# A vision block on one core: queries and keys of the first attention projected once and put into blocks by transfers, with new lists

## The reference

```
h  = [cls, rfft2(16x16 patches).real * freq weights @ proj] + pos      # 197 tokens of 192
x1 = layernorm(h)
q, k, v = x1 @ Wq + bq, x1 @ Wk + bk, x1 @ Wv + bv                     # 12 heads of 16
h  = h + concat(softmax(q @ k.T / 4) @ v) @ Wo + bo
x2 = layernorm(h)
gates = softmaxes and a top-2 choice of x2 @ (wg, wg0, wg1)            # a factor for each of 12 heads
q, k, v = x2 @ qkv_w + qkv_b                                           # 12 heads of 64
o  = softmax(layernorm(q) / 8 @ layernorm(k).T) @ v
h  = h + (gates * o) @ proj_w + proj_b
```

## Time and profile before

| | |
|---|---|
| median of three runs | 5198.48 us |
| the profiled execution | 5189.76 us, its span 5188.0 us |
| granted TensorE clock, mean | 0.996 |
| busy share TensorE, weight loads, DVE, ACT, POOL | 97%, 82%, 90%, 85%, 66% |
| DMA | 131.44 MB, 25 GB/s over the span |

### The profile page before, as it was taken

How to read it: one execution, slowest core, us unless ns; L and a number is a source line. 1 busy time by engine, 2 the same in 40 slices (tenths; PEclk the granted TensorE clock), 3 DMA queues, 4 the chain that set the end, 5 groups by cost and what they waited for, 6 DMA issues and landing times.

```text
span 5188.0 us, 196660 instructions
## 1 busy us (share of the span) xinstructions
PE 5021.8 (97%) x61744; PEld 4268.3 (82%) x61744; DVE 4664.9 (90%) x14799; ACT 4402.2 (85%) x17537; POOL 3434.1 (66%) x3462
## 2 busy tenths in 40 slices
...
GB/s 90 20 26 22 22 29 22 22 29 22 22 23 28 22 22 29 22 22 29 22 22 23 29 22 22 29 22 22 29 22 22 22 29 22 22 29 22 22 25 6
DMA packets 69030, 131.44 MB, mean 25 GB/s; under 512 B 8628, under 2 KB 34624, under 8 KB 68704
## 3 DMA queue, kind: packets, MB, share of 16 engines
...
...
## 4 chain that ended last, share of the span: by engine, by line
PE 52%; DVE 35%; issue 11%; DVEq 1%; ACT 0%; POOL 0%; POOLq 0%; ACTq 0%
PE bank L528 42%; PE bank L705 9%; DVE nmax L948 6%; DVE nmax L1047 4%; DVE qkn L1042 4%; DVE v L1024 2%; DVE gfac L1013 2%; DVE qk L943 2%; DVE x L918 2%; DVE oT L1065 2%; DVE h L970 1%; DVE stats L905 1%; DVE ctxT L1060 1%; DVE vs L960 1%; DVE parts L921 1%
## 5 line engine op out<-in xcount | busy, mean ns | idle before, releaser
L512 POOL TENSOR_TENSOR pq<-pq,gn 99x788 f32<-99x788 f32 x768 | 1151.9, 1500 | 756.0 <-DVE gn L1056 742.4
L773 ACT ACTIVATE p<-bank,nmax 99x197 f32<-99x197 f32 x3072 | 1283.5, 438 | 219.4 <-DVE nmax L948 219.4
L811 ACT ACTIVATE pq<-bank,nmax 99x197 f32<-99x197 f32 x3072 | 1287.3, 447 | 137.8 <-DVE nmax L1047 137.8
L1047 DVE TENSOR_REDUCE nmax<-bank 99x2 f32<-99x394 f32 x1536 | 829.8, 561 | 131.0 <-PE bank L528 131.0
L516 POOL TENSOR_TENSOR sq<-qkc 128x396 f32<-128x396 f32 x768 | 644.5, 846 | 364.1 <-ACT qkc L785 364.0
L948 DVE TENSOR_REDUCE nmax<-bank 99x2 f32<-99x394 f32 x1536 | 821.3, 564 | 41.7 <-PE bank L528 38.7
L817 ACT ACTIVATE pT<-bank 99x394 f32<-99x394 f32 x1536 | 740.5, 526 | 66.0 <-PE bank L705 65.9
L528 PE MATMUL bank<-x2T,wqkc 128*128 128x198 f16 (+1 forms) x7680 | 734.1, 249 | 5.7 <-ACT p L773 4.7
L528 PEld LDWEIGHTS bank<-x2T,wqkc 128*128 128x128 f16 (+1 forms) x7680 | 654.8, 98 | 79.6 <-DVE x2T L980 41.0
L705 PE MATMUL bank<-ident,pq 99*99 99x99 f32 (+1 forms) x6144 | 709.6, 254 | 9.0 <-POOL pq L512 7.7
L811 ACT ACTIVATION_READ_ACCUMULATOR pq<-bank,nmax 99x1 f32 x3072 | 700.7, 228 | 0.0
(11 more groups left out here) (155 smaller groups left out, 10335.6 us busy)
## 6 DMA issues: line engine op xcount, KB each, us to landing
xa<-in_xa SPq DMA_DIRECT2D x128, 392.0 KB, 3.1
xb<-in_xb SPq DMA_DIRECT2D x128, 392.0 KB, 3.7
out_tokens<-res SPq DMA_DIRECT2D x128, 74.2 KB
out_tokens<-res SPq DMA_DIRECT2D x128, 73.5 KB
...
```

Source lines behind the costliest of these rows:

```text
L512: nc.gpsimd.tensor_tensor(pair, pair, factor, op=ALU.mult).then_inc(s_sc.up(), 1)
L773: last = nc.scalar.activation(p1[0:TC, h, c, :], psum("s1", h)[0:TC, c * T:c * T + T], ACT.Exp, bias=nmax1[:, c, h:h + 1], accum_out=sum1[ ...
L811: last = nc.scalar.activation(pq[0:TC, h % SLOTS, c, 0:T], psum("s2", h)[0:TC, c * T:c * T + T], ACT.Exp, bias=nmax2[:, h, c:c + 1], accum ...
L1047: V.tensor_reduce(nmax2[:, h, :], psum("s2", h)[0:TC, 0:2 * T].rearrange("p (a b) -> p a b", a=2), op=ALU.max, axis=AX.X, negate=True).the ...
```

## The change

The weights of queries and keys are held once: for a group of four heads 64 columns of queries, then 64 of keys. A qk1 step is one set of five matmuls. ACT writes the high parts of both, DVE the low parts, into a new tile qkhl. When all three groups are there, SP copies qkhl into the blocks of the tile qk1 by 16 transfers within SBUF: for each of the four heads of a group and each half of its 32 rows, one transfer of the queries (high and low, three groups, 16 rows of 3 x 792 bytes) and one of the keys (high for the first half, low for the second, 16 rows of 3 x 396 bytes). Each head has a semaphore, and every s1 step waits for all four. ACT, before it writes qkhl, waits that the transfers of the image before are done and that its s1 steps on TensorE are.

All five lists are new, banks included; SP's gains an entry qx between load and store. Before the loop, ACT makes the high parts of the weights and DVE the low ones; one load of weights goes, and the clearing of v2 moves ahead of the loads.

```
 ORDER = {
     "pe": """
+1:o2_0@0 1:pT_3@5 4:tok@3 2:qk1@6 1:s2_10@05 1:pT_4@2 2:qk2@1 1:pT_5@6 2:qk3@3 3:s1_4@0724 1:o2_1@6 1:o2_2@1 2:qk4@3
+1:pT_6@5 2:qk5@0 1:pT_7@7 3:ctx0@3 2:ms0@0 2:ms1 2:ms2 3:s1_8@2751 1:o2_3@3 1:pT_8@6 2:v2_0@4 1:pT_9@2 3:ctx1@6
+1:pT_10@7 2:rstd0@2 4:x1T@0 2:rstd1@4 1:pT_11@7 1:o2_4@2 1:o2_5@4 2:s2_0@63 2:rstd2@2 4:qk1_0@0 2:v2_1@7 2:v2_2@5
+2:v2_3@1 2:rstd3@4 4:qk1_1@0 3:ctx2@6 2:s2_2@21 4:qk1_2@3 4:v1@0 3:wo@4 2:s2_4@57 1:proj@3 2:pT_0@4 2:rstd4@6 2:pT_1@0
+3:x2T@2 2:s2_6@45 2:rstd5@6 3:qk0@2 2:pT_2@0 4:s1_0@3617 2:s2_8@24
     "dve": """
+4:tok 1:s2_10 1:s2_11 1:gr4 3:ctx0 3:s1_4 3:s1_5 4:nx1 1:ol1 3:s1_6 1:gr5 3:s1_7 1:ol2 3:cl0 3:s1_8 3:s1_9 3:s1_10
+3:ctx1 2:var2 2:v2_0 2:rstd0 2:rstd1 3:cl1 3:s1_11 1:ol3 4:x1T 1:ol4 3:ctx2 2:s2_0 2:rstd2 2:s2_1 1:ol5 4:qk1_0 2:v2_1
+2:v2_2 2:v2_3 2:gl 2:rstd3 2:gate1 4:qk1_1 3:cl2 2:s2_2 2:gate2 2:gate3 2:gr0 4:qk1_2 3:wo 2:s2_3 2:s2_4 3:nx2 2:gr1
+2:rstd4 2:s2_5 3:x2T 2:s2_6 2:rstd5 1:proj 2:s2_7 4:s1_0 4:s1_1 2:s2_8 2:gr2 4:s1_2 2:ol0 4:s1_3 2:s2_9 2:gr3
...
     "sp": """
-4:load 0:store
+4:load 3:qx 0:store
...
-        wqk1 = sb("wqk1", [128, 4, 2 * 3 * 128], F16)
+        wqk1 = sb("wqk1", [128, 4, 3 * 128], F16)
-        qk1 = sb("qk1", [128, 3, 2, 2, TP], F16)
+        qk1 = sb("qk1", [128, 3, 3, TP], F16)
+        qkhl = sb("qkhl", [128, 3, 2, TP], F16)
+        s_qx = [signal(f"qk1_blocks{j}", 64) for j in range(GROUP)]
...
+            def qk_blocks(img, _):
+
+                sp.wait_ge(*read_out(img, "qk1", 2))
+                for j in range(GROUP):
+                    for half in range(2):
+                        dst = slice(32 * j + 16 * half, 32 * j + 16 * half + 16)
+                        sp.dma_start(qk1[dst, :, 0:2, :], qkhl[16 * j:16 * j + 16]).then_inc(s_qx[j].up(16), 16)
+                        sp.dma_start(qk1[dst, :, 2, :], qkhl[64 + 16 * j:80 + 16 * j, :, half, :]).then_inc(s_qx[j].up(16), 16)
+
+            run_phases(sp, "sp", {"qx": qk_blocks, "load": load, "store": store})
...
-                for s in range(2):
-                    w = slice(128 * (3 * s + g), 128 * (3 * s + g) + 128)
-                    last = mm5(o[:, s * TP:s * TP + TP], lambda k, r: wqk1[r, k, w], lambda k, r: x1T[r, k].rearrange("p c n -> p (c n)"), True)
+                w = slice(128 * g, 128 * g + 128)
+                last = mm5(o[:, 0:TP], lambda k, r: wqk1[r, k, w], lambda k, r: x1T[r, k].rearrange("p c n -> p (c n)"), True)
...
-                pe.wait_ge(*read_out(img, "qk1", h // GROUP))
+                for j in range(GROUP):
+                    pe.wait_ge(*s_qx[j].at(img, 64))
...
+            def high_parts(source, dest):
+
+                nc.scalar.activation(dest[:, 0:2], source[:, 0:2], ACT.Copy, scale=W_SCALE)
+                nc.scalar.activation(dest[:, 3], source[:, 2], ACT.Copy, scale=row_scale[:, 0:1]).then_inc(s_high, 1)
...
-                nc.scalar.activation(qk1[:, g, 0, 0, :], psum("qk1", g)[:, 0:TP], ACT.Copy, scale=E1 ** -0.25 / W_SCALE)
-                nc.scalar.activation(qk1[:, g, 0, 1, :], psum("qk1", g)[:, TP:2 * TP], ACT.Copy,
-                                     scale=mask1[:, 0:1]).then_inc(s_qkh.up(), 1)
+                for j in range(GROUP):
+                    act.wait_ge(*s_qx[j].at(img, 0))
+                if not isinstance(img, int) or img > 0:
+                    for h in range(H - GROUP, H):
+                        act.wait_ge(*made(img - 1, "s1", h))
+                nc.scalar.activation(qkhl[:, g, 0, :], psum("qk1", g)[:, 0:TP], ACT.Copy, scale=E1 ** -0.25 / W_SCALE).then_inc(s_qkh.up(), 1)
...
             def split(source, dest):
 
-                link(V.tensor_scalar(dest[:, 0:2], source[:, 0:2], W_SCALE, None, ALU.mult))
-                link(V.tensor_scalar(dest[:, 3], source[:, 2], W_SCALE, bias_rows[:, 0:1], ALU.mult, ALU.mult))
-                link(V.scalar_tensor_tensor(dest[:, 2], source[:, 0], W_SCALE, dest[:, 0], ALU.mult, ALU.subtract))
-                link(V.scalar_tensor_tensor(dest[:, 3], source[:, 2], W_SCALE, dest[:, 3], ALU.mult, ALU.subtract))
+                high[0] += 1
+                dve.wait_ge(s_high, high[0])
+                V.scalar_tensor_tensor(dest[:, 2], source[:, 0], W_SCALE, dest[:, 0], ALU.mult, ALU.subtract)
+                V.scalar_tensor_tensor(dest[:, 3], source[:, 2], W_SCALE, dest[:, 3], ALU.mult, ALU.subtract)
...
-                V.scalar_tensor_tensor(qk1[:, g, 1].rearrange("p a b -> p (a b)"), psum("qk1", g)[:, 0:2 * TP], E1 ** -0.25 / W_SCALE,
-                                       qk1[:, g, 0].rearrange("p a b -> p (a b)"), ALU.mult, ALU.subtract).then_inc(free("qk1", g), 1)
+                V.scalar_tensor_tensor(qkhl[:, g, 1, :], psum("qk1", g)[:, 0:TP], E1 ** -0.25 / W_SCALE,
+                                       qkhl[:, g, 0, :], ALU.mult, ALU.subtract).then_inc(free("qk1", g), 1)
```

More of the change, by code:

```diff
@@ L155 @@
-1:s2_0 3:ctx0 1:s2_1 1:rstd3 0:ol4 2:nx2 3:qk1_1 1:v2_1 1:v2_2 1:rstd4 3:qk1_2 0:ol5 1:v2_3 1:s2_2 2:x2T 3:s1_4 1:s2_3
-1:gl 3:s1_5 1:gate1 1:gate2 1:gate3 3:s1_6 3:cl0 1:gr0 3:s1_7 1:s2_4 1:s2_5 1:gr1 4:tok 1:s2_6 1:s2_7 4:nx1 1:gr2
-0:proj 3:s1_8 3:s1_9 3:s1_10 1:rstd5 3:s1_11 3:ctx1 1:ol0 1:s2_8 1:s2_9 4:x1T 3:ctx2 1:gr3 1:ol1 1:s2_10 3:cl1
+4:tok 1:s2_10 1:s2_11 1:gr4 3:ctx0 3:s1_4 3:s1_5 4:nx1 1:ol1 3:s1_6 1:gr5 3:s1_7 1:ol2 3:cl0 3:s1_8 3:s1_9 3:s1_10
+3:ctx1 2:var2 2:v2_0 2:rstd0 2:rstd1 3:cl1 3:s1_11 1:ol3 4:x1T 1:ol4 3:ctx2 2:s2_0 2:rstd2 2:s2_1 1:ol5 4:qk1_0 2:v2_1
@@ L158 @@
+2:v2_2 2:v2_3 2:gl 2:rstd3 2:gate1 4:qk1_1 3:cl2 2:s2_2 2:gate2 2:gate3 2:gr0 4:qk1_2 3:wo 2:s2_3 2:s2_4 3:nx2 2:gr1
+2:rstd4 2:s2_5 3:x2T 2:s2_6 2:rstd5 1:proj 2:s2_7 4:s1_0 4:s1_1 2:s2_8 2:gr2 4:s1_2 2:ol0 4:s1_3 2:s2_9 2:gr3
 """,
     "act": """
-0:pT_2 0:pT_3 2:s1_8 2:s1_9 2:s1_10 0:o2_0 1:qk4 2:s1_11 1:qk5 0:o2_1 3:x1T 0:s2_8 0:s2_9 2:ctx1 1:var0 1:var1 0:pT_4
-0:s2_10 3:qk1_0 2:ctx2 0:pT_5 0:s2_11 3:v1 0:pT_6 0:o2_2 0:pT_7 0:pT_8 3:s1_0 0:o2_3 3:s1_1 3:s1_2 0:pT_9 0:pT_10
-0:pT_11 3:s1_3 0:o2_4 0:o2_5 1:s2_0 3:qk1_1 4:xhi 1:s2_1 3:qk1_2 2:x2T 1:s2_2 3:s1_4 3:ctx0 1:gate0 1:s2_3 2:qk0
@@ L163 @@
-3:s1_5 2:qk1 3:s1_6 2:qk2 3:s1_7 1:s2_4 1:s2_5 1:pT_0 2:qk3 1:pT_1 1:s2_6 1:s2_7
+0:pT_10 2:s1_10 0:pT_11 3:x1T 0:o2_4 2:s1_11 0:o2_5 4:xhi 3:qk1_0 1:s2_0 1:s2_1 1:gate0 3:qk1_1 2:ctx2 3:qk1_2 1:s2_2
+1:s2_3 3:v1 1:s2_4 1:pT_0 1:pT_1 2:x2T 1:s2_5 1:s2_6 2:qk0 1:pT_2 1:s2_7 3:s1_0 3:s1_1 1:o2_0 1:pT_3 1:s2_8 3:s1_2
+3:s1_3 1:s2_9 2:qk1 1:pT_4 1:s2_10 1:pT_5 2:qk2 1:s2_11 2:qk3 3:s1_4 1:o2_1 3:s1_5 2:qk4 1:o2_2 1:pT_6 2:qk5 3:s1_6
+1:pT_7 3:ctx0 3:s1_7 2:var0 3:s1_8 2:var1 1:pT_8 3:s1_9 1:pT_9 3:ctx1 1:o2_3
@@ L398, in build_vit_block @@
         s_prep = ctx.enter_context(nc.semaphore("prep_vector_step"))
+        s_high = ctx.enter_context(nc.semaphore("weights_high_parts"))
+        s_centred = ctx.enter_context(nc.semaphore("weights_centred"))
         s_pw = ctx.enter_context(nc.semaphore("token_weights_scaled"))
@@ L405, in build_vit_block @@
                        (bias_rows[:], "bias_rows"), (mask1[:], "mask1")]
[L406 removed]
+        first_loads = [(wq1_raw, "wqk1"), (wv1_raw, "wv1"), (wgate_raw, "wgate")]
         second_loads = [(wq_raw, "wq"), (wk_raw, "wk")]
@@ L832, in _ @@
             V.memset(parts[1][:], 1.0)
-            for x in (vs1, ctxT, pq, oT, xh, xl):
+            for x in (vs1, ctxT, pq, oT, xh, xl, v2):
                 V.memset(x[:], 0.0)
@@ L885, in _ @@
             link(V.tensor_scalar(ln_b[:, 0:1], ln_b[:, 0:1], E2 ** -0.5, None, ALU.mult))
-            link(V.memset(v2[:], 0.0))
             dve.wait_ge(s_weff, 6 * KC)
```

52 lines of the change are left out of this document (32 added, 20 removed).

## The result

The changed kernel takes 6024.12 us (median of six runs, 6022.86 to 6025.69), the kernel before 5198.58 beside it: the ratio is 1.1588, interval 1.1573 to 1.1603. The direction was right, the size was not: +826 us where +30 was forecast.

The account below looks back on a forecast made before the run. The prediction took a loop through PE, DVE and SP's transfers as the bound: 15.4 + 15.8 + 7.8 + 0.3 + 0.3 = 39.6 us an image against 39.33, +38 us, less 9 before the loop: 5228 us, range 5110 to 5400.

Parts of the forecast that it names:

- a loop from the third qk1 over SP's transfers to s1_0: Main loop across PE, DVE and SP, closed by the transfers: claimed to set the period at 39.6 us an image.
- DVE's leg: DVE's work from s1_8 to the third qk1 step, put at 15.8 us an image.
- The preparation: Weight preparation before the loop, where ACT takes high parts from DVE: -9 us, bounds 0 to -13.
- The transfers: SP's 16 issues after the third qk1 plus the last landing: 7.8 us, from 7.1 to 12.9.
- the wait that I did forecast: PE at s1_0 waiting for the transfers to land, put at about 0.7 us an image.
- PE's start after the landing: Hand-over from the last transfer's landing to PE's s1_0, estimated at 0.1 us.
- the first term: Time of SP's 16 transfers, issues and last landing, in the loop's sum: 7.8 us, bounds 7.1 to 12.9.
- the second rival: Transfers are dearer, 0.47 us an issue and 2.4 to land, 9.45 in all: 5445 us; chance 0.15.
- PE's total: PE's busy time an image, forecast to fall by 1.3 us from 38.9 to 37.6 through halved projections.
- the third rival: PE bounds the kernel throughout and gives back all that it saves: 5019 us; chance 0.05.
- the first rival: Transfers are hidden, 0.36 us an issue and 7.1 in all: 38.9 us an image, 5138 us; chance 0.32.
- the cover: DVE's steps after the third qk1 until proj, whose bank s1_0 needs, hiding the transfers: 7.1 us.

Follow-up runs that it names:

- the dummies: Changed kernel with 36 matmuls an image that nothing reads, placed ahead of s1_0's wait for the transfers; 5710.41 us, ratio 1.1008.

## Why the prediction was wrong

**Right.** That the end hangs on a loop from the third qk1 over SP's transfers to s1_0, over PE to s1_8 and over DVE back: each link stands in the trace, and taking transfers, DVE steps or the clock's fall out of it moved the time by about the amount that the loop says, as far down as PE's own 38.9 us an image. DVE's leg: 15.8 and 0.1 for the hand-over to SP, 15.9 measured. A qk1 step on PE: 0.435, 0.43 measured (3050.80 to 3051.23). DVE's low parts, by form:

```profile
L980 DVE SCALAR_TENSOR_TENSOR qkhl<-bank,qkhl 128x198 f16<-128x198 f32 x384 | 138.9, 362 | 21.0 <-ACT qkhl L795 5.9
```

against 562 ns in the earlier trace rows. The preparation: -9 us forecast, -12.4 at the memset here and -11 by its own run.

**Wrong.** What failed is the price of an issue, and beside it a term put at nothing, TensorE's clock. By the terms of the sum, 39.6 forecast and 46.6 measured in the image that was read:
1. *The transfers*, 15 x 0.41 + 1.66 = 7.8: measured 15 x 0.64 + 1.9 = 11.5, +3.7 us. The 0.41 came from two HBM loads; a transfer within SBUF takes at least half as long again to issue, whatever its size, and no row of the kernel before has one. The landing was nearly right.
2. *TensorE's clock*, not in the sum at all: the wait that I did forecast, grown from 0.7 to 4.6 us, brings PE back at 1.2 GHz. s1_0 to s1_8 was put at 15.4, with 0.3 for added waits and 0.1 for the hand-over to DVE; it takes 16.0 at full clock and 18.7 as it ran: +2.9, of which 2.7 are the clock (2.2 in the mean of the images).
3. *PE's start after the landing*, 0.1 forecast, 0.5 measured: +0.4. With the dummies ahead of it, it is 0.1.

3.7 + 2.9 + 0.4 = 7.0, the difference between 46.6 and 39.6.

The range failed by a choice of mine, not for want of a row. The bounds of the first term reached 12.9 us, from 0.65 an issue, which lay nearer to the truth than the value I took. Carried through, 12.9 is 39.6 + 5.1 = 44.7 us an image, about 5880, without the clock. The range stopped at 5400, inside the second rival. The sign that the prediction asked for in that rival (issues 0.5 or more apart) was there; its price, 9.45 us for the transfers, was still 2 us short.

Two lesser steps. PE's total did not fall to 37.6 us but stayed at 38.9: the lists spent the 1.3 us saved, so that the third rival's 5019 was out of reach whatever the transfers cost, and the first rival's 5138 would have been 5177, as the run without transfers shows. And the cover is 7.75 us, 0.6 more than I added up: by an estimate from 0.64 an issue and 1.9 to land, enough for ten transfers, not for sixteen. The Trainium skill ("DMA: Bandwidth & Descriptors", Issuing engines are not separate DMA queues) says that issuing from several engines saves only the sequencer's time of initiation, usually small beside the transfer itself. For one transfer that is so here, 0.64 us against 1.9 to land; sixteen in a row on one queue make 9.6 us, and these decide.

Still open: why an issue within SBUF costs 0.64 us and one with HBM at an end 0.40 to 0.46, why two steps of one kind in a row are cheaper on PE than apart, and what, beside the length of the wait, decides how much of an image PE works at the low clock.
